# Folding the variance's scale and 1e-5 into ScalarE's square root in a two-layer decoder kernel

## The reference

```python
def _layernorm(x, axis=-1, eps=1e-05):
    m = jnp.mean(x, axis=axis, keepdims=True)
    v = jnp.var(x, axis=axis, keepdims=True)
    return (x - m) / jnp.sqrt(v + eps)

# layer 1, self attention: 16 query heads, 4 key/value heads, D = 128
    def _layernorm(x, g, b):
        mu = jnp.mean(x, axis=-1, keepdims=True)
        var = jnp.mean(jnp.square(x - mu), axis=-1, keepdims=True)
        return (x - mu) * jax.lax.rsqrt(var + EPS) * g + b
...
    q = _layernorm(q, qn_g, qn_b)
    k = _layernorm(k, kn_g, kn_b)
    q = q * cos + _rotate_half(q) * sin
    k = k * cos + _rotate_half(k) * sin
...
x = x + _L0_attn_ref(_layernorm(x, axis=-1), ...)     # RWKV time mix
x = x + _L0_xattn_ref(_layernorm(x, axis=-1), ...)    # attention over 1601 context rows
x = x + _L0_ffn_ref(_layernorm(x, axis=-1), ...)      # 8 experts, top 1
x = x + _L1_attn_ref(_layernorm(x, axis=-1), ...)     # grouped-query attention
x = x + _L1_xattn_ref(_layernorm(x, axis=-1), ...)
x = x + _L1_ffn_ref(_layernorm(x, axis=-1), ...)      # 16 experts, top 2
```

## Time and profile before

| | us |
|---|---|
| median of three timed runs | 1526.54 |
| lowest and highest | 1518.20, 1528.69 |
| profiled execution | 1517.35 |
| its span | 1515.6 |

### The profile page before, as it was taken

One profiled execution on the slowest core, in us unless ns is written; L12 is line 12 of the kernel. 1 busy time (PEld: TensorE's weight loads), 2 busy tenths in 40 slices (PEclk: granted clock), 3 DMA queues, 4 the chain that ended last, 5 costly groups with the idle time before them and its releaser, 6 DMA issues.

```text
span 1515.6 us, 21060 instructions
## 1 busy us (share of the span) xinstructions
PE 1384.6 (91%) x7568; PEld 904.4 (60%) x7568; DVE 909.2 (60%) x1615; ACT 642.2 (42%) x1630; POOL 860.8 (57%) x766
## 2 busy tenths in 40 slices
PE   6579998999999999999998576998999989989998
PEld 3466554555555555555557553445777855578887
DVE  6855666566666666666642527996664126656555
ACT  2320112344444444444440323887663238834332
POOL 4415001588988988888891434887442016615554
PEclk9787999899999999999999787998999999989999
DMA  9300111000000000000007220000000042000000
GB/s 251 108 1 9 34 35 42 5 11 8 8 9 10 8 8 11 8 8 11 8 4 254 77 80 19 1 1 1 1 1 25 1 121 71 1 1 1 1 1 29
DMA packets 53375, 48.64 MB, mean 32 GB/s; under 512 B 18048, under 2 KB 49688, under 8 KB 52760
## 3 DMA queue, kind: packets, MB, share of 16 engines
q1 hardware_dynamic: 52504, 45.20, 10.8%
q0 software_dynamic: 768, 2.10, 0.4%
HBM read 34.18 MB, written 4.72 MB: 26 GB/s over the span
## 4 chain that ended last, share of the span: by engine, by line
PE 78%; DVE 9%; ACT 6%; POOL 3%; issue 2%; DMA 1%; SPq 0%; DVEq 0%; POOLq 0%; ACTq 0%
PE PS L436 73%; PE PS L444 4%; ACT s_sc L1131 2%; DVE s_mx L1542 1%; ACT a_m L1089 1%; DVE r_den L1285 1%; POOL a_m L1735 1%; DVE HN L1235 1%; PE PS L580 1%; POOL a_m L1729 1%; ACT a_sq L1098 1%; ACT QKT L947 1%; DVE pm L1363 1%; DVE r_den L1282 1%; POOL PWS L1676 0%
## 5 line engine op out<-in xcount | busy, mean ns | idle before, releaser
L1676 POOL TENSOR_TENSOR PWS<-PWS 128x1024 f32<-128x1024 f32 x160 | 379.8, 2374 | 68.6 <-ACT PWS L1029 52.4
L1029 ACT ACTIVATE PWS<-PS 128x512 f32<-128x512 f32 (+1 forms) x416 | 227.8, 595 | 277.2 <-PE PS L436 264.6
L1363 DVE TENSOR_REDUCE pm<-PS 128x2 f32<-128x1024 f32 x192 | 227.4, 1221 | 77.0 <-PE PS L436 76.5
L436 PE MATMUL PS<-PWS,KVR 128*64 128x256 f32 (+1 forms) x1664 | 206.7, 386 | 0.0
L436 PE MATMUL PS<-QALL,KH 128*128 128x512 f32 (+1 forms) x416 | 187.2, 450 | 1.5 <-ACT PWS L1029 1.5
L436 PE MATMUL PS<-QM,KL 68*128 68x512 f32 (+1 forms) x416 | 166.0, 399 | 0.0
L436 PEld LDWEIGHTS PS<-PWS,KVR 128*64 128x64 f32 (+1 forms) x1664 | 109.5, 136 | 85.8 <-issue 34.5
L1750 POOL TENSOR_SCALAR s_sc<-s_sc,s_ri 128x128 f32<-128x128 f32 (+1 forms) x256 | 104.0, 425 | 93.3 <-DVE s_ri L1549 93.3
L436 PEld LDWEIGHTS PS<-QALL,KH 128*128 128x128 f32 (+1 forms) x416 | 77.6, 186 | 72.2 <-issue 35.9
L1131 ACT ACTIVATE s_sc<-PS,s_nb 128x128 f32<-128x128 f32 (+1 forms) x256 | 104.4, 433 | 4.5 <-DVE s_nb L1545 4.5
L1542 DVE TENSOR_REDUCE s_mx<-PS 128x2 f32<-128x512 f32 (+2 forms) x112 | 65.7, 611 | 48.2 <-PE PS L436 48.2
(11 more groups left out here) (279 smaller groups left out, 2858.7 us busy)
## 6 DMA issues: line engine op xcount, KB each, us to landing
QALL<-qlo SPq DMA_DIRECT2D x32, 128.0 KB, 2.4
QM<-QALL SPq DMA_DIRECT2D x64, 64.0 KB, 2.0
f_w<-in_L_ffn_w_dram SPq DMA_DIRECT2D x2, 2048.0 KB
a_nat<-in_L_attn_w_qkv_dram SPq DMA_DIRECT2D x1, 3072.0 KB, 21.5
x_wq<-in_L_xattn_Wq_dram SPq DMA_DIRECT2D x1, 2048.0 KB, 9.6
x_wo<-in_L_xattn_Wo_dram SPq DMA_DIRECT2D x2, 1024.0 KB, 7.0
a_wo<-in_L_attn_w_o_dram SPq DMA_DIRECT2D x1, 2048.0 KB, 20.9
m_wd<-in_L_ffn_Wd_dram SPq DMA_DIRECT2D x1, 2048.0 KB, 8.5
```

Of the source, the lines that this page charges most:

```text
L436: return nc.tensor.matmul(o, a, b, start=start, stop=stop, **kw)
L1029: nc.scalar.activation(PW[c][0:rows, j * HALF:(j + 1) * HALF], PS[0:rows, k % 2 * 512:(k % 2 + 1) * 512], ACT.Exp).then_inc(p_ready, 1)
L1363: ins = V.tensor_reduce(pm[u % 2][:, :, i // 3, i % 3], src, AX, ALU.max)
L1676: G.tensor_tensor(ACC[:, :], PW[0][:, :] if i == 0 else ACC[:, :], PW[i + 1][:, :], ALU.add).then_inc(acc_step, 1)
```

## The change

In the heads' norm, VectorE's L1521 goes away, and with it its wait for the reduction and the semaphore `hvar_ready`. The square root reads the sum of squares directly and does scale and addition itself, as sqrt(sum / 128 + 1e-5), with the scale as an immediate and the bias from a column of SBUF (`guard`). ScalarE now waits for the semaphore by which the reduction frees the bank. In all layer norms L1231 goes away as well: the root reads the variances in `mv` (every second column) with the bias from `guard`, and the last of the four aggregations raises `var_ready`. The column is set by one more memset at GpSimd's start, for which ScalarE waits once, ahead of its first root.

```diff
-        pool_tick = sb("pool_tick", [P, 8])
+        guard = sb("guard", [P, 8])
@@ deviations
                 act.wait_ge(var_ready, 2 * k + g + 1)
-                nc.scalar.activation(rstd[:, 4 * g:4 * g + 4], rstd[:, 4 * g:4 * g + 4], ACT.Sqrt).then_inc(std_ready, 1)
+                nc.scalar.activation(rstd[:, 4 * g:4 * g + 4], mv[:, 4 * g:4 * g + 4, 1], ACT.Sqrt,
+                                     bias=guard[:, 0:1]).then_inc(std_ready, 1)
@@ start of ScalarE's list
+            act.wait_ge(guard_set, 1)
             for g in range(2):
                 deviations(0, g)
@@ ScalarE, stage 6
                     if n >= 2:
-                        act.wait_ge(hvar_ready, n - 1)
+                        act.wait_ge(*banks.emptied(("qkv", (n - 2) // 5, (n - 2) % 5)))
                     nc.scalar.activation(a_sq[:, n % 2, :], banks.bank(key), ACT.Square).then_inc(sq_ready, 1)
                 if 1 <= n <= 5 * NT:
-                    act.wait_ge(hvar_ready, n)
-                    nc.scalar.activation(a_ss[:, (n - 1) % 4, :], a_ss[:, (n - 1) % 4, :], ACT.Sqrt).then_inc(hstd_ready, 1)
+                    act.wait_ge(*banks.emptied(("qkv", (n - 1) // 5, (n - 1) % 5)))
+                    nc.scalar.activation(a_ss[:, (n - 1) % 4, :], a_ss[:, (n - 1) % 4, :], ACT.Sqrt, bias=guard[:, 0:1],
+                                         scale=1.0 / P).then_inc(hstd_ready, 1)
@@ normalise
                 for t in tiles:
                     dve.wait_ge(dve_step, steps[0] - 3 + t - 4 * g)
-                    V.bn_aggr(mv[:, t, :], stats[:, t, :]).then_inc(dve_step, 1)
-                steps[0] += 4
-                dve.wait_ge(dve_step, steps[0])
+                    ins = V.bn_aggr(mv[:, t, :], stats[:, t, :])
+                ins.then_inc(var_ready, 1)
                 r = rstd[:, 4 * g:4 * g + 4]
-                V.tensor_scalar(r, mv[:, 4 * g:4 * g + 4, 1], LN_EPS, None, ALU.add).then_inc(var_ready, 1)
@@ parts
                                 ALU.add).then_inc(emptied["dve"], 1)
-                dve.wait_ge(*banks.emptied(key))
-                V.tensor_scalar(a_ss[:, n % 4, :], a_ss[:, n % 4, :], 1.0 / P, LN_EPS, ALU.mult, ALU.add).then_inc(hvar_ready, 1)
@@ start of GpSimd's list
             link(G.memset(r_ones[:, :], 1.0))
+            G.memset(guard[:, 0:1], LN_EPS).then_inc(guard_set, 1)
```

More of the change, by code:

```diff
@@ L307, in decoder @@
         std_ready = sem("deviations_ready")
-        hvar_ready = sem("head_variances_ready")
         hstd_ready = sem("head_deviations_ready")
@@ L314, in decoder @@
         ones_set = sem("ones_set")
+        guard_set = sem("variance_guard_set")
         w_exp = sem("rwkv_exp_ready")
```

## The result

| | before | changed |
|---|---|---|
| first comparison, median of 6 and 6 runs | 1526.74 | 1515.37 |
| lowest and highest | 1518.20, 1528.69 | 1512.77, 1518.67 |
| second comparison, median of 29 and 12 runs | 1520.31 | 1515.98 |
| span of the profiled execution | 1515.6 | 1516.9 |

The first comparison gives a ratio of 0.994, with a 95% interval of 0.9911 to 0.9968, the second 0.9973 (0.9956 to 0.999). So the changed kernel is faster by well under 1%, 11 us in the first pair and 4.3 in the second, against a prediction of 4.0 (1522.5 on the median, with a range of 1510 to 1530). The two profiled executions even stand the other way round, at mean granted clocks of 0.946 (before) and 0.941 (changed). What the change itself did is therefore read stage by stage first, and the 11 us later.

A forecast was written before the change was run, and what follows sets the result against it. TensorE, on 78% of the chain, was taken as the bound, the seam's chain hiding most of the saving. Beginning 0.6, six tiles 1.0, end 1.6 and norms 0.8 sum to 4.0 us: median 1526.54 to 1522.5, range 1510 to 1530.

The forecast's parts named there:

- The loop over GpSimd: In the projection stage, L1521's 0.75 us read as waiting for GpSimd's L1729, making VectorE's pitch of 2.73 a loop.
- The seam's chain of 8.80: TensorE's turn to turn across two token tiles: 8.80 us for three groups, with neither L1518 nor L1521 in it.
- only engine times count: Rival: the seam's latency closes up and TensorE bounds the stage, 12.5 us a tile against 14.2, giving 1512; chance 0.08.
- Inside the tile: Steps of a token tile away from the seam: GpSimd decides with 2.46 us a group, a gain of 0.25.
- the double copy: ScalarE's two copies (values and queries) at a tile's first group: 2.71 us before, 2.7 to 2.8 between squares expected after.
- Six tiles: Six token tiles between like places in the projection stage: 1.0 us gained in all, bounds 1.0 to 1.5.
- The bias's price: A root with its bias from SBUF takes 0.09 us more, leaving a tile 0.16 gained instead of 0.25.
- The beginning of the stage: Start of the projection stage, before any seam: third group's L1729 and first turn come earlier, 0.6 us gained (0 to 0.7).
- The end of the stage: Four groups after the last seam: last square root about 1.7 us earlier, gain 1.6 (0.7 to 1.7).
- The norms: L1231 removed in the layer norms: 0.11 us in each of seven half norms on the path, 0.8 (to 1.4).
- The first norm: Root's table loads later, halves come some 1.1 us later; cost 0, covered by TensorE's first weights until 15.30.
- The sum: Whole kernel: 0.6 + 1.0 + 1.6 + 0.8 = 4.0 us gained, median 1522.5; 0 to 6 gained had chance 0.83.

The follow-up runs named there:

- heads_only: The changed kernel with the six layer norms put back as before, so only the heads' norm is changed: 1518.42 us, ratio 0.9993 against before.
- before_copy: The kernel before, unchanged, run against itself on one chip: median 1523.01 us against 1525.83, ratio 0.9994.
- norms_only: The changed kernel with the heads' norm put back as before, only the layer norms changed: 1525.60 us, ratio 1.0029; repeated on another chip 1524.19, 0.9989.
- idle_scalar: The changed kernel plus one TENSOR_SCALAR of 128x4 behind each head group's reduction, for which nobody waits: 1526.55 us, one run.
- before_values_first: The kernel before with ScalarE's copy of the values moved ahead of the next tile's first square: 1522.49 us, one run.
- lag_five: The changed kernel with the values' copy ahead of the next tile's first square and TensorE turning group n-5, not n-4: 1501.68 us, ratio 0.9871 against before.

## Why the prediction was right, and where it was off

- **The loop over GpSimd** in the earlier trace rows was read rightly: an instruction that nobody waits for costs the same 0.23 a tile when it is a TENSOR_SCALAR, and nothing when it is a reciprocal. One detail was off and didn't matter: VectorE's own pitch, where nothing holds it, is 1.95 in the changed kernel (931.20 to 933.15), where I had 2.06.
- **The seam's chain of 8.80** in the earlier trace rows stayed at 8.81, with and without L1521, and is what hid the change: once it was lengthened to four groups, with the values' copy moved, the tile fell to 12.5, the time I had given to the rival "only engine times count". That rival was wrong for this change and right for the kernel with the longer chain.
- **Inside the tile** GpSimd took over with 2.46, as worked out, and the double copy with 2.80. The tile is 14.07 against 14.05. Six tiles gave (1026.00 - 940.75) - (1025.64 - 941.24) = 0.85, where I had 1.0.
- **The bias's price** of 0.09 from the earlier trace rows is measured at 91 ns (298 against 207). A tile gained 0.14 with it and 0.23 without, where I had 0.16 and 0.25.
- **The beginning of the stage** was undersized. I had 0.6, at most 0.7. From the first square to the sixth it is 14.22 before, and 12.97, 13.50 and 13.48 in the changed kernel, its repeat and heads_only, so 0.7 to 1.25 less. I followed one group there, and L1521 had held up each of the first four. But 14.22 is the low figure of the old code: before_copy took 15.67, norms_only 15.93 and 15.63, idle_scalar 15.92. TensorE's first turn and the two products behind it, in before and then in norms_only:

```profile
936.62 0.66 PE L444 MATMUL PS<-ident,a_m 128*128 128x128 f32 x4 [2.27 <-POOL a_m L1735]
937.12 3.60 PE L436 MATMUL PS<-a_wT,HT 128*128 128x512 f32 x8
```

```profile
939.01 0.66 PE L445 MATMUL PS<-ident,a_m 128*128 128x128 f32 x4 [2.75 <-POOL a_m L1737]
939.50 5.29 PE L437 MATMUL PS<-a_wT,HT 128*128 128x512 f32 x8
```

  After the wait of 2.75 the granted clock fell from 1.00 to the lower level (0.57 in 940 to 944), and the same two products took 5.29 in place of 3.60. Such a fall, of some 3 us, stands here in all four of the profiles just named: norms_only (two), before_copy and idle_scalar, with waits of 2.75, 3.32, 3.32 and 2.76. It is not in before and before_values_first (2.27 and 2.25), nor in the six profiles that have neither L1521 nor an idle TENSOR_SCALAR and still wait there (1.48 to 1.56), nor in the two kernels with the turn of n-5, which don't wait. Against the executions with the fall the beginning gained 2.1 to 3.0, so L1521 seems to cost more at this place than its own delay in some of them. That the longer wait brings the fall is read from these profiles and was not tested, and every run has but one profile, so how often it happens is not known.
- **The end of the stage:** 20.98 to 19.38, a gain of 1.60, as predicted. From the square of group 35 to the last root it is 14.24 before (1026.00 to 1040.24) and 12.55 now (1025.64 to 1038.19), 1.69 less, where I had 1.7.
- **The norms:** from the last four aggregations to the reciprocal, in the second half of the second norm, it was 0.84 (82.28 to 83.12) and is 0.73 (80.53 to 81.26), 0.11 a half norm. For all of them the runs give 0.3 (+-0.6), which can't tell 0.8 from nothing.
- **The first norm:** its cover held, as shown above.
- **The sum:** 4.0 predicted. The profiled stage alone gained 3.7 (3.1 to 5.1 over the two profiles of each kernel), the second comparison 4.3 and the fit at equal clock 2.9 (+-0.7). The first comparison gained 11.4, to a median of 1515.37, 7 us below the 1522.5 that I had. Its runs of before carry no clock in the record, but five of six lie at 1526.5 to 1528.7, and in the other series before lies at 1525.3 to 1529.3 when its clock is 0.938 or 0.939, while five of the changed kernel's six had 0.944 to 0.947. So some 8 of the 11 us fit a difference of clock (from 0.9385 to 0.946 would be 9, an estimate by the slope above). What stays open is why: a chance of the series, as with norms_only, or something in the changed timing that draws a higher clock (median 0.946 over the 18 runs of two series against 0.943). The fall at the first turn is one place where the timing could do so, but 3 us at half the clock are only 0.001 of the mean. The runs don't decide it. That 1515.37 lies in the range is in part luck: the terms of the sum were sized about right, but the clock was not among them, and the range was wide enough only because it took the spread between executions as its width.

## What to carry to other kernels

An instruction removed from a busy engine gives back its time only in those steps of the loop where no other chain ends later. Walk one whole period, seams included, and note for each step what releases it. If the longest chain doesn't pass the removed instruction, give that chain more slack first: here the same removal was worth 0.14 us a tile before and 1.25 after. And compare runs of a TensorE-bound kernel at equal granted clock before taking a few us for an effect, but look also at whether the change itself moves the clock somewhere, since that comparison leaves it out.

## What the runs showed of the hardware that I had not expected

- A small TENSOR_SCALAR from SBUF to SBUF (128x4, 0.17 alone) stood for 0.75 to 0.86 us in VectorE's queue next to GpSimd's additions of 1.27, though its data were free; a RECIPROCAL of the same size and place took 0.166, and the TENSOR_REDUCE of 128x512 0.67 with and without it.
- The mean granted clock of executions of one program on one chip went from 0.937 to 0.949 (before, 17 runs beside lag_five), and 0.001 of it goes with 1.23 us in this kernel. That is more than all of this change, and it comes in stretches such as 30 us at the lower level in heads_only, where another execution had the full clock in the same 30 us. TensorE had been waiting, with 8.12 busy of 10 us, in the stretch ahead of the fall.
- Waits of TensorE of 2.75 to 3.32 us ahead of its first turn in stage 6 went, in all four profiles that show them, with some 3 us at the lower clock at their end or behind them, and the two products there took 4.60 to 5.30 in place of 3.60.
